# Attention scores of two heads side by side in 64-row halves of TensorE, from two float32r parts

## The chip, the core and the metric

The kernel runs on one core of a Trainium2 chip. The metric is the device time of one launch in microseconds. In the views, PE is TensorE (PEld its weight loads), DVE is VectorE, ACT is ScalarE, POOL is GpSimd and SP is SyncE, whose queue issues the DMAs.

## The reference

One transformer layer with the norms behind: 1024 tokens, width 512, 32 query heads of 16 channels in 8 groups (4 query heads share the keys and values of a group), causal attention, then a linear layer with eight LoRA terms.

```python
q = jnp.dot(x, Wq).reshape(b, t, H, HD).transpose(0, 2, 1, 3)        # H = 32, HD = 16, t = 1024
kv = jnp.dot(x, Wkv).reshape(b, t, G, 2, HD).transpose(2, 3, 0, 1, 4) # G = 8
scores = jnp.einsum('bhqd,bhkd->bhqk', q, k)
scores = jnp.where(causal[None, None], -jnp.inf, scores)
weights = jax.nn.softmax(scores * (1.0 / HD ** 0.5), axis=-1)
ctx = jnp.einsum('bhqk,bhkd->bhqd', weights, v)
# attention: jnp.dot(ctx, Wo) + bo, and then
h = jnp.einsum('bsd,nrd->nbsr', x, lora_A)
coef = (SCALE * lora_weights)[:, None, None]
lora_out = jnp.einsum('nbsr,nor->bso', h, lora_B * coef)
base = jnp.einsum('bsd,od->bso', x, W) + bias
# x = _layernorm(x + attention), then x = _layernorm(x + base + lora_out)
```

## The kernel before

All inputs are float32 and the result is held to float32 accuracy, so narrow types are split into parts whose products are summed. Projections, the output product (WO) and the FFN (FF) take operands in two float32r parts, three products each (`halves`, line 1195). For the scores, query and key are split into three bfloat16 parts, and six products of parts stand below each other as 6 x 16 = 96 rows of the contraction (`ROWS`), so that one matmul of 96 rows makes the scores of a head in full accuracy. `QS` holds these rows for the four heads of a unit, `KS` for the keys of a group. Three more rows (`NROW` = 99) hold the negative row maximum in three bfloat16 parts against rows of ones, so that the scores of the softmax come out with the maximum already subtracted.

The work is cut into 16 units: a unit `u` is four heads of a group and one half (512) of the queries. Units 0 to 7 take the first half, 8 to 15 the second, which sees twice the keys. Each unit passes twice over its scores:

- **Chunks** (`CHUNKS`, `chunk_scores`, line 1135) make scores with the query on the partitions, one matmul a head, up to 512 keys wide. DVE reduces each PSUM bank to a maximum (`chunk_max`: line 910 for a full bank, the fused operation of line 917 with the causal mask for one head of an "own" bank). They run one to three cycles ahead. They take turns in banks 0 to 2 and, where nothing else holds it, bank 7.
- **Cycles** (`CYCLES`, 80 of them) make the scores again with the key on the partitions (`piece_scores`, line 1359, 512 columns each), ACT takes their exponential into `PB` (line 856), on the diagonal POOL zeroes the part above it (line 696), and `accumulate` (line 1337) multiplies `PB` with the values in float32, four heads side by side in 32-column strips of the array. A cycle has four pieces off the diagonal and three on it. A piece has one of the banks 3 to 5 (`ST_BANKS` = 3; from the last unit on six banks).

The order on each engine is written out by the program. TensorE goes through a cycle in four steps, each with a share of the chunks, a piece and a share of the **filler** (`FILL`), the part of another job that goes on beside: projections of the second half, and the T1, T2, WO, T3, FF steps behind the attention of the first half. `accumulate` of the cycle before closes it. How many chunks each cycle takes is planned by `level` from `pe_time` and `dve_time`.

The unit's maxima go DVE (line 931) -> POOL in three parts (`split_maxima`) -> TensorE turns them (line 1143) -> ACT copies (line 744) -> a DMA puts them into `QS` (`move_maxima`, line 507). The first unit does without the DMA: `direct_rows` and `rows_moved` write them straight from PSUM.

A projection of queries or keys ends in `parts`: ACT copies the high part (line 732), DVE subtracts it (line 958), ACT makes the middle part (line 737), POOL the low one (line 582; DVE does it for the first two, line 968). SP then writes `parts` to DRAM (`parts_to_dram`, line 479), waits until it has landed and reads it back in the layout of the rows (`load_queries`, `load_keys`). SP works through this queue strictly in order. The first unit's rows are made by selection matmuls instead (line 1149).

## Time and profile before

| | |
|---|---|
| median of 3 runs | 341.34 us (339.17 to 341.63) |
| the profiled execution: its time, its span | 339.0 us, 337.2 us |
| PE busy | 322.3 us (96%), 2487 matmuls |
| DVE busy | 256.6 us (76%) |
| ACT busy | 216.5 us (64%) |
| POOL busy | 135.3 us (40%) |
| granted clock of TensorE | 0.996 of 2.4 GHz |

Busy time counts a matmul from its issue to its end; matmuls overlap in the pipeline, so a busy PE may still be issuing below its rate. The stages used below are cut at the end of a unit's last `accumulate`: until 36 us the loads, first projections and first chunks, until 100.7 us units 0 to 4, until 128.4 us units 5 to 7, until 265.2 us units 8 to 13 (22.8 us each), until 303.1 us units 14 and 15, then the tail of the second half's WO and FFN. The times of all runs outside the span are 339.0 - 337.2 = 1.8 us.

### The profile page before, as it was taken

How to read it: one execution, taken by the hardware profiler on the slowest of the kernel's cores; microseconds unless marked ns; L12 is line 12 of the kernel's file. 1: busy time of each engine (PE TensorE's matmuls, PEld its weight loads, DVE VectorE, ACT ScalarE, POOL GpSimd, SP SyncE). 2: the span in 40 equal slices, each digit the busy share in tenths (PEclk: the TensorE clock that was granted, in tenths of full speed). 3: DMA queues.
4: the chain of work that ended last, by engine and by line, in shares of the span. 5: the costliest groups of instructions: out<-in, count | busy, mean ns of one | idle time of the engine just before them, and what ended most of it. 6: DMA issues, size and time to landing. Idle time of an engine off the chain costs nothing.

```text
span 337.2 us, 7240 instructions
## 1 busy us (share of the span) xinstructions
PE 322.3 (96%) x2487; PEld 169.7 (50%) x2487; DVE 256.6 (76%) x787; ACT 216.5 (64%) x418; POOL 135.3 (40%) x268
## 2 busy tenths in 40 slices
PE   8999989999999999999999999999999999999992
PEld 3676445455353344454444544544544434558882
DVE  3557968978888899888889889888886961047664
ACT  4754737645657796848757668478585786952431
POOL 8845325433547585347222123212141122331553
PEclk9999999999999999999999999999999999999998
DMA  6886494874244120020010100000000000000002
GB/s 202 289 163 170 132 183 120 225 230 118 53 148 155 36 63 5 3 47 3 3 48 33 48 4 3 0 31 3 3 0 3 32 2 1 2 33 1 0 33 93
DMA packets 16643, 22.96 MB, mean 68 GB/s; under 512 B 3232, under 2 KB 10560, under 8 KB 16608
## 3 DMA queue, kind: packets, MB, share of 16 engines
q1 hardware_dynamic: 16608, 22.51, 24.4%
q8 instruction: 20, 0.33, 0.4%
q14 instruction: 15, 0.12, 0.1%
HBM read 16.29 MB, written 6.03 MB: 66 GB/s over the span
## 4 chain that ended last, share of the span: by engine, by line
PE 71%; DMA 7%; DVE 7%; ACT 4%; issue 4%; SPq 3%; POOL 2%; POOLq 0%; DVEq 0%; ACTq 0%
PE PS L1337 18%; PE PS L1195 16%; PE PS L1135 15%; PE PS L1359 15%; DMA QS<-NMR 3%; ACT PB L856 2%; PE PS L1263 2%; PE PS L1255 2%; DVE scrap L917 2%; DVE MX L910 2%; DMA scr_q<-parts 2%; DMA X<-in_L_attn_x_turned_dram 1%; SPq L490 1%; PE PS L1149 1%; SPq L502 1%
## 5 line engine op out<-in xcount | busy, mean ns | idle before, releaser
L856 ACT ACTIVATE PB<-PS 128x512 f32<-128x512 f32 x288 | 155.6, 604 | 59.1 <-PE PS L1359 57.9
L917 DVE CUSTOM_DVE_ANT_0 scrap<-PS,mask 128x128 bf16<-128x128 f32 (+3 forms) x256 | 111.5, 487 | 17.6 <-PE PS L1135 17.1
L1135 PE MATMUL PS<-KS,QS 96*128 96x512 bf16 (+3 forms) x384 | 107.9, 329 | 2.1 <-DVE MX L910 1.0
L1359 PE MATMUL PS<-QS,KS 99*128 99x512 bf16 x288 | 106.2, 381 | 1.8 <-DMA QS<-NMR 1.4
L910 DVE TENSOR_REDUCE MX<-PS 128x1 f32<-128x512 f32 x128 | 81.9, 684 | 12.4 <-PE PS L1135 11.7
L696 POOL TENSOR_SCALAR_AFFINE_SELECT PB<-PB 128x256 f32<-128x256 f32 (+1 forms) x96 | 46.4, 485 | 104.3 <-ACT PB L856 101.2
L1337 PE MATMUL PS<-PB,VX 128*32 128x256 f32 (+1 forms) x1280 | 78.8, 364 | 0.6 <-ACT PB L856 0.3
L1135 PEld LDWEIGHTS PS<-KS,QS 96*128 96x128 bf16 x384 | 32.9, 98 | 49.4 <-issue 13.6
L1337 PEld LDWEIGHTS PS<-PB,VX 128*32 128x32 f32 x1280 | 33.5, 109 | 41.9 <-issue 19.0
L1195 PE MATMUL PS<-XT,WQ 128*128 128x512 f32 x144 | 45.4, 439 | 0.5 <-ACT NMR L744 0.4
L1359 PEld LDWEIGHTS PS<-QS,KS 99*128 99x128 bf16 x288 | 27.5, 98 | 31.4 <-ACT PB L856 7.9
L1195 PEld LDWEIGHTS PS<-XT,WQ 128*128 128x128 f32 x144 | 26.6, 193 | 9.5 <-DVE XT L1043 1.5
L1195 PE MATMUL PS<-XT 128*128 128x512 f32 x96 | 28.1, 426 | 0.6 <-DVE MX L910 0.6
L1195 PE MATMUL PS<-WQ,XT 128*128 128x512 f32 x96 | 28.3, 427 | 0.0
L677 POOL TENSOR_SCALAR mv<-mv 128x1 f32<-128x1 f32 x15 | 3.4, 228 | 48.7 <-DVE mv L1012 48.6
L917 DVE DVE_READ_ACCUMULATOR2_ANT MX<- 128x1 f32 x256 | 21.2, 83 | 0.0
L1195 PEld LDWEIGHTS PS<-XT 128*128 128x128 f32 x96 | 17.9, 189 | 4.6 <-DVE MX L910 1.1
L1195 PEld LDWEIGHTS PS<-WQ,XT 128*128 128x128 f32 x96 | 17.9, 189 | 4.1
L770 ACT ACTIVATE RAW<-PS 128x256 f32<-128x256 f32 x32 | 12.4, 387 | 11.2 <-PE PS L1337 11.0
L788 ACT ACTIVATE TC<-RAW,shift,rstd 128x512 f32<-128x512 f32 x7 | 5.7, 817 | 13.4 <-POOL shift L679 13.4
L732 ACT ACTIVATE parts<-PS 128x512 bf16<-128x512 f32 x10 | 6.0, 597 | 10.7 <-PE PS L1195 10.7
L658 POOL CAST NMPS<-NM 128x16 bf16<-128x16 f32 x15 | 3.3, 221 | 21.7 <-DVE NM L931 21.7
(93 smaller groups left out, 263.6 us busy)
## 6 DMA issues: line engine op xcount, KB each, us to landing
scr_q<-parts SPq DMA_DIRECT2D x8, 384.0 KB, 4.0
QS<-scr_q SPq DMA_DIRECT2D x15, 192.0 KB, 2.9
X<-in_L_attn_x_turned_dram SPq DMA_DIRECT2D x8, 256.0 KB, 6.3
X<-in_L_attn_x_dram SPq DMA_DIRECT2D x8, 256.0 KB, 3.1
out_dram<-TC SPq DMA_DIRECT2D x8, 256.0 KB, 2.0
QS<-scr_q SPq DMA_DIRECT2D x15, 128.0 KB, 3.0
RAW<-in_L_attn_Wo_dram SPq DMA_DIRECT2D x2, 512.0 KB, 5.9
RAW<-in_L_ffn_W_dram SPq DMA_DIRECT2D x2, 512.0 KB, 9.0
```

The costliest lines, as they stand in the source:

```text
L696: nc.gpsimd.affine_select(out=blk, in_=blk, compare_op=ALU.is_ge, fill=0.0, base=0, pattern=[[0, len(heads)], [1, P]], channel_multiplier=-1)\
L732: nc.scalar.activation(parts[:, m % 2, 0, :], job_bank(n), ACT.Copy).then_inc(act_copied, 1)
L770: nc.scalar.activation(RAW[:, u, cols], PS[:, PV_BANK, cols], ACT.Copy).then_inc(raw_out, 1)
L856: nc.scalar.activation(PB[:, cyc % NP_BUF, k, :], PS[:, score_bank(e), :], ACT.Exp, scale=SCALE)\
L910: nc.vector.tensor_reduce(part[:, j0:j1, 0:1], bank, AX, ALU.max).then_inc(max_read, 1)
L917: last = nc.vector.tensor_tensor_reduce(out=scrap[:, n % 2, (j - j0) * width:(j - j0 + 1) * width], in0=bank[:, j - j0, :], in1=mask[:, HT ...
L1135: last = nc.tensor.matmul(PS[:, CHUNK_BANK[n], k * width:(k + 1) * width], QS[0:ROWS, u % SLOTS, j, qb * P:(qb + 1) * P], KS[0:ROWS, g, k0 ...
L1195: last = nc.tensor.matmul(bank, lhs(a, c), rhs(b, c), start=(k == 0), stop=(k == len(terms) - 1))
L1255: last = nc.tensor.transpose(bank[:, g * P:(g + 1) * P], RAW[:, h * G + g0 + g, qb * P:(qb + 1) * P], ident[:, :])
L1263: last = nc.tensor.transpose(bank[:, c * P:(c + 1) * P], src[:, c * P:(c + 1) * P], ident[:, :])
L1337: last = nc.tensor.matmul(PS[32 * j:32 * j + 32, PV_BANK, s * HQ + skip:(s + 1) * HQ], VX[:, key_blocks(cyc)[i], u % G, :], PB[:, cyc % NP ...
L1359: nc.tensor.matmul(PS[:, score_bank(e), :], KS[0:NROW, u % G, kb * P:(kb + 1) * P], QS[0:NROW, u % SLOTS, heads[0]:heads[-1] + 1, s * HQ + ...
```

## The change

- Query and key are split into two float32r parts instead of three bfloat16 ones. Three products (high x high, high x low, low x high) take 3 x 16 = 48 rows, 51 with the maxima. The middle part on ACT and the low part on POOL (and on DVE for the first two jobs) are gone.
- The 51 rows fit in 64. Of a unit's four heads two stand in rows 0 to 50 and two in rows 64 to 114 of `QS`. `KS` has the keys of one group in the upper and of another in the lower half, and a unit takes two heads of each (`v_group`, and `Wq` and `Wo` are laid out for it ahead of the launch).
- Chunks and pieces are issued in pairs, the first in rows 0 to 63 of the array, the second in rows 64 to 127, into two different banks, with one semaphore increment for both; each pair waits until both banks are free. All score matmuls have float32r operands.
- On the diagonal the one piece of four heads is two pieces of 256 columns, so a cycle has always four pieces; ACT and POOL have four operations there instead of three.
- A long filler comes in two parts of six matmuls, at the first and last step of a cycle, instead of four parts of three; a short one in one part at the last step.
- The first unit's maxima take the DMA as all others do: `move_maxima(0)` stands in SP's queue behind the five `parts_to_dram`, and TensorE waits for it ahead of cycle 0. 16 chunks are due ahead of cycle 0 instead of 14.
- `load_queries` has four DMAs of 2 KB rows for three of 4 KB, `load_keys` four for six, `move_maxima` two for three. `parts` has 512 KB for 384.
- Ones are written into all of `KS` before anything is copied into it, so the copies and loads wait for that constant. In the tail the banks are dealt out anew.

```diff
-    ROWS = 6 * HD
+    ROWS = 3 * HD
     NROW = ROWS + NPART
+    PAIR, TILE = 2, 64
+    Q_TERMS, K_TERMS = (0, 0, 1), (0, 1, 0)
+    def tile_rows(t, count):
+        return slice(t * TILE, t * TILE + count)
+    def v_group(u, j):
+        return (u % G) // 2 + G // 2 * (j // 2)
...
         first = [(0, range(0, 2), 0), (0, range(2, 4), 0)]
-        return first + ([(1, range(0, 4), P)] if on_diagonal(cyc) else [(1, heads, 0) for _, heads, _ in first])
+        return first + [(1, heads, P if on_diagonal(cyc) else 0) for _, heads, _ in first]
...
-        return HT * len(pieces(c)) * (1 + 1.1) / 2.4 + (PE_FILL.get(kind, 2600) if kind else 0)
+        return HT * len(pieces(c)) * (0.6 + 1.1) / 2.4 + (PE_FILL.get(kind, 2600) if kind else 0)
...
-        QS = sb("QS", [P, SLOTS, REP, HT], BF16)
-        KS = sb("KS", [P, G, T], BF16)
+        QS = sb("QS", [P, SLOTS, NPAIR, HT], F32R)
+        KS = sb("KS", [P, G // 2, T], F32R)
...
-        parts = sb("parts", [P, 2, NPART, HT], BF16)
+        parts = sb("parts", [P, 2, 2, HT], F32R)
...
-            load_keys(1, slice(0, G), ks_in[1])
+            move_maxima(0)
+            load_keys(1, slice(0, G // 2), ks_in[1])
...
                 if on_diagonal(cyc):
-                    for k, (_, heads, _) in enumerate(pieces(cyc)):
+                    for k, (_, heads, skip) in enumerate(pieces(cyc)):
...
-            def middle_part(n):
-
-                act.wait_ge(*freed(PROJ[n]))
-                nc.scalar.activation(parts[:, n % 2, 1, :], rest[:, n % 2, :], ACT.Copy).then_inc(rest_split, 1)
...
-                    nc.vector.tensor_tensor(rest[:, s, :], bank, parts[:, s, 0, :], ALU.subtract)\
+                    nc.vector.tensor_tensor(parts[:, s, 1, :], bank, parts[:, s, 0, :].bitcast(F32), ALU.subtract)\
                         .then_inc(job_freed, 1)
...
                 was_read(CHUNK_BEHIND[n])
-                for k, j in enumerate(heads):
-                    last = nc.tensor.matmul(PS[:, CHUNK_BANK[n], k * width:(k + 1) * width],
-                                            QS[0:ROWS, u % SLOTS, j, qb * P:(qb + 1) * P],
-                                            KS[0:ROWS, g, k0:k0 + width], start=True, stop=True)
+                was_read(CHUNK_BEHIND[n + 1])
+                for k in range(len(CHUNKS[n][3])):
+                    for t in range(PAIR):
+                        j = CHUNKS[n + t][3][k]
+                        rows = tile_rows(t, ROWS)
+                        last = nc.tensor.matmul(PS[:, CHUNK_BANK[n + t], k * width:(k + 1) * width],
+                                                QS[rows, u % SLOTS, j % NPAIR, qb * P:(qb + 1) * P],
+                                                KS[rows, v // 2, k0:k0 + width], start=True, stop=True)
                 last.then_inc(max_scores, 1)
...
-                if not long and head % 2 == 0:
+                if head not in ((0, 3) if long else (3,)):
                     return
-                part, parts = (head, REP) if long else (head // 2, 2)
+                part, parts = (head // 3, 2) if long else (0, 1)
...
-                nc.tensor.matmul(PS[:, score_bank(e), :], KS[0:NROW, u % G, kb * P:(kb + 1) * P],
-                                 QS[0:NROW, u % SLOTS, heads[0]:heads[-1] + 1, s * HQ + skip:(s + 1) * HQ],
-                                 start=True, stop=True).then_inc(scores, 1)
+            def pair_scores(cyc, i):
+
+                u, s, _ = CYCLES[cyc]
+                kb = key_blocks(cyc)[i]
+                e = SCORE_BANKS[cyc] + PAIR * i
+                for t in range(PAIR):
+                    bank_free(e + t)
+                for t in range(PAIR):
+                    _, heads, skip = pieces(cyc)[PAIR * i + t]
+                    rows = tile_rows(t, NROW)
+                    last = nc.tensor.matmul(PS[:, score_bank(e + t), 0:len(heads) * (HQ - skip)],
+                                            KS[rows, (u % G) // 2, kb * P:(kb + 1) * P],
+                                            QS[rows, u % SLOTS, :, s * HQ + skip:(s + 1) * HQ], start=True, stop=True)
+                last.then_inc(scores, 1)
...
-                if cyc == 0:
-                    rows_moved()
-                elif cyc == FIRST[u]:
-                    pe.wait_ge(nm_in, 16 * NPART * u)
+                if cyc == FIRST[u]:
+                    pe.wait_ge(nm_in, 16 * PAIR * (u + 1))
```

The order on TensorE in the same cycle (the one in which WO of the first block is the filler, unit 9). Before:

```order
L1337 MATMUL PS<-PB,VX 32x256 x8
L1135 MATMUL PS<-KS,QS 128x256 x2
L1359 MATMUL PS<-QS,KS 128x512
L1195 MATMUL PS<-WQ,XT 128x512 x3
L1135 MATMUL PS<-KS,QS 128x512 x2
L1359 MATMUL PS<-QS,KS 128x512
L1195 MATMUL PS<-WQ,XT 128x512 x3
L1135 MATMUL PS<-KS,QS 128x512
L1359 MATMUL PS<-QS,KS 128x512
L1195 MATMUL PS<-WQ,XT 128x512 x3
L1135 MATMUL PS<-KS,QS 128x512
L1135 MATMUL PS<-KS,QS 128x384
```

And in the changed kernel, where line 1118 is the chunks, 1330 the pieces, 1159 the fillers and 1301 `accumulate`:

```order
L1301 MATMUL PS<-PB,VX 32x256 x8
L1330 MATMUL PS<-QS,KS 128x512 x2
L1159 MATMUL PS<-WQ,XT 128x512 x6
L1118 MATMUL PS<-KS,QS 128x256 x4
L1118 MATMUL PS<-KS,QS 128x512 x2
L1330 MATMUL PS<-QS,KS 128x512 x2
L1118 MATMUL PS<-KS,QS 128x512 x2
L1159 MATMUL PS<-WQ,XT 128x512 x6
L1301 MATMUL PS<-PB,VX 32x256 x4
```

Four single pieces between fillers of three have become two pairs, with a filler of six behind the first and another ahead of `accumulate`.

SP's queue at the start of the attention, from the write of the fourth projection on. Before (line 479 `parts_to_dram`, 502 `load_queries`, 490 `load_keys`, 512 `move_maxima`):

```order
L479 DMA scr_q<-parts 128x3x512
L502 DMA QS<-scr_q 48x2048
L502 DMA QS<-scr_q 32x2048
L502 DMA QS<-scr_q 16x2048
L479 DMA scr_k<-parts 128x3x512
L490 DMA KS<-scr_k 16x8x512 x6
L512 DMA QS<-NMR 1x16x128 x3
```

And in the changed kernel (lines 484, 513, 498, 521 in the same order):

```order
L484 DMA scr_q<-parts 128x2x512
L513 DMA QS<-scr_q 16x1024
L513 DMA QS<-scr_q 32x1024
L513 DMA QS<-scr_q 16x1024
L513 DMA QS<-scr_q 32x1024
L484 DMA scr_k<-parts 128x2x512
L521 DMA QS<-NMR 3x8x128 x2
L498 DMA KS<-scr_k 32x4x512
```

The maxima move of the first unit is new and stands ahead of the keys of the second half, with four query loads where three were. Ahead of these rows stand the write of the third projection and the query loads of two units, now eight DMAs for six.

## Rows read from the trace of the kernel before

**Rows 1.** Busy us (instructions) of PE, PEld, DVE, ACT, POOL by stage; clock; DMA.

```profile
0.00:36.00 36.00, 33.84 (x153) 21.04 (x154) 21.65 (x65) 19.50 (x33) 23.90 (x37) 1.00 0.72 198
36.00:100.70 64.70, 60.86 (x474) 30.63 (x472) 55.20 (x235) 38.86 (x80) 26.19 (x61) 1.00 0.59 155
100.70:128.40 27.70, 27.03 (x245) 11.40 (x234) 25.29 (x76) 22.55 (x49) 20.93 (x35) 1.00 0.28 79
128.40:265.20 136.80, 135.58 (x1158) 65.67 (x1147) 118.41 (x331) 95.75 (x185) 41.13 (x88) 1.00 0.05 14
265.20:303.10 37.90, 36.89 (x347) 18.09 (x337) 14.76 (x40) 29.45 (x58) 10.16 (x23) 1.00 0.04 15
```

**Rows 2.** Groups by line and form: busy us, mean ns, idle before.

```profile
L856 ACT ACTIVATE PB<-PS 128x512 f32<-128x512 f32 x288 | 155.6, 604 | 59.1 <-PE PS L1359 57.9
...
L1337 PE MATMUL PS<-PB,VX 128*32 128x256 f32 x1024 | 71.8, 386 | 0.6 <-ACT PB L856 0.3 <-ACT RAW L770 0.2
...
L1195 PEld LDWEIGHTS PS<-XT,WQ 128*128 128x128 f32 x144 | 26.6, 193 | 9.5 <-DVE XT L1043 1.5 <-ACT NMR L744 1.3 <-ACT XT L815 1.0
...
L770 ACT ACTIVATE RAW<-PS 128x256 f32<-128x256 f32 x32 | 12.4, 387 | 11.2 <-PE PS L1337 11.0
...
L1263 PEld LDWEIGHTS PS<-ident,TC 128*128 128x128 f32 x64 | 8.2, 141 | 4.1 <-DVE MX L910 0.6 <-DVE TC L981 0.4
```

**Rows 3.** The stage 128.4 to 265.2, maxima score matmuls of line 1135 alone.

```profile
128.40:265.20 136.80, 58.89 (x192) 17.02 (x192) 1.00 0.05 14
```

**Rows 4.** The same stage, softmax score matmuls of line 1359 alone.

```profile
128.40:265.20 136.80, 59.42 (x156) 15.25 (x156) 1.00 0.05 14
```

**Rows 5.** The same stage, projection and FFN matmuls of line 1195 alone.

```profile
128.40:265.20 136.80, 25.09 (x72) 13.60 (x72) 1.00 0.05 14
```

**Rows 6.** Chain of waits in order of time: start us, us, what.

```profile
273.63 0.22 PE PS L1263 x2
...
277.24 0.86 PE PS L1359 x4
278.10 1.00 PE PS L1337 x16
279.10 0.32 PE PS L1359
...
281.28 1.38 PE PS L1195 x6
```

**Rows 7.** The same view, early: 128 and 256 columns of line 1135.

```profile
20.40 0.24 PE PS L1135 x4
...
21.63 0.23 PE PS L1135 x2
```

**Rows 8.** Waits, 128.4 to 265.2: who for whom, us, times, longest.

```profile
ACT PB L856 <- PE PS L1359: 33.6, 42, 2.6
...
DVE MX L910 <- PE PS L1135: 10.2, 21, 1.3
```

**Rows 9.** Busy time in the 20 us where VectorE is fullest.

```profile
120.00:140.00 20.00, 19.88 (x181) 8.75 (x178) 18.71 (x55) 16.12 (x33) 12.07 (x19) 1.00 0.08 22
```

**Rows 10.** Timeline of the DMA queue of SyncE: start us, us, what.

```profile
26.09 0.38 SPq L479 DMA_DIRECT2D scr_q<-parts  x1
28.66 2.64 SPq L502 DMA_DIRECT2D QS<-scr_q  x6
31.34 0.42 SPq L479 DMA_DIRECT2D scr_q<-parts  x1
35.30 1.23 SPq L502 DMA_DIRECT2D QS<-scr_q  x3
...
43.94 1.86 SPq L512 DMA_DIRECT2D QS<-NMR  x3
```

**Rows 11.** Timeline of GpSimd, the low part of one projection.

```profile
24.89 1.17 POOL L582 TENSOR_TENSOR parts<-TC,parts 128x512 bf16<-128x512 f32 x1 [1.65 <-ACT parts L737]
```

**Rows 12.** Timeline of TensorE, the first softmax scores.

```profile
36.04 0.38 PE L1359 MATMUL PS<-QS,KS 99*128 99x512 bf16 x1
```

More of the change, by code:

```diff
@@ L15 @@
 EPS = 1e-5
-ONE_ONE = float(np.array([0x3F803F80], np.uint32).view(np.float32)[0])
 ALPHA = 32
@@ L75, in postln_kernel @@
     LAST_OF = {last_of(u, s): (u, s) for u in range(NU) for s in range(2)}
-    def heads_per_bank(width):
-        return min(REP, HT // width) if width <= HT // 2 else 1
     def heads_in_banks(width):
-        n = heads_per_bank(width)
-        return [range(j, j + n) for j in range(0, REP, n)]
+        if width <= HT // 2:
+            return [range(0, 2), range(2, 4)]
+        return [range(j, j + 1) for j in (0, 2, 1, 3)]
     CHUNKS = []
@@ L133, in chunks_of_job @@
         before, due = PLAN_A[n - 1][1] if n else 0, PLAN_A[n][1]
-        a, b = (before + (max(before, due) - before) * p // 3 for p in (part, part + 1))
+        a, b = (before + (due - before) // 2 * p // 3 * 2 for p in (part, part + 1))
         return range(a, b)
@@ L152, in postln_kernel @@
     assert list(FILL) == sorted(FILL)
-    POOL_AT = {c + 1: [("low", PROJ.index(job))] for c, job in FILL.items() if job in PROJ}
+    POOL_AT = {}
     for b in range(TB):
@@ L194, in level @@
             done += r
-            due.append(sum(1 for n in chunks if COST[n + 1] - COST[chunks[0]] <= done + 1))
+            due.append(2 * sum(1 for n in chunks[::2] if COST[n + 2] - COST[chunks[0]] <= done + 1))
         due[-1] = len(chunks)
@@ L275, in postln_kernel @@
     LATE = [(e - WIDE) % ALL_BANKS for e in range(SCORE_BANKS[NCYC - 1], SCORE_BANKS[NCYC])]
-    FREE = [bank for bank in range(ALL_BANKS) if bank not in LATE] + [MISC]
+    FREE = [bank for bank in range(ALL_BANKS) if bank not in LATE] + [MISC, LATE[0]]
+    LATE = LATE[1:]
     assert len(LATE) == 3 and len(FREE) == 4
@@ L852, in _ @@
                     evacuate(*LAST_OF[cyc - 2])
-                for k in range(len(pieces(cyc))):
+                for k, (_, heads, skip) in enumerate(pieces(cyc)):
                     e = SCORE_BANKS[cyc] + k
-                    act.wait_ge(scores, e + 1)
-                    nc.scalar.activation(PB[:, cyc % NP_BUF, k, :], PS[:, score_bank(e), :], ACT.Exp, scale=SCALE)\
-                        .then_inc(probs, 1)
+                    width = len(heads) * (HQ - skip)
+                    act.wait_ge(scores, e // PAIR + 1)
+                    nc.scalar.activation(PB[:, cyc % NP_BUF, k, 0:width], PS[:, score_bank(e), 0:width], ACT.Exp,
+                                         scale=SCALE).then_inc(probs, 1)
                     if k == 0 and cyc == rows_cycle(1) + 1:
@@ L1146, in direct @@
             def direct(lhs, slot, bank):
-                for a in range(NPART):
-                    last = nc.tensor.matmul(PS[0:ROWS, bank, :], lhs[:, a, :], parts[:, slot, a, :],
-                                            start=(a == 0), stop=(a == NPART - 1))
+                for a in range(2):
+                    last = nc.tensor.matmul(PS[:, bank, :], lhs[:, a, :], parts[:, slot, a, :], start=(a == 0),
+                                            stop=(a == 1))
                 last.then_inc(moved, 1)
             def direct_keys():
-                pe.wait_ge(parts_ready, 1)
+                pe.wait_ge(*freed(("K", 0, 0)))
                 pe.wait_ge(sel_ready, 12)
@@ L1295, in _ @@
                     pe_job(n, part)
-                    for k in chunks_of_job(n, part):
+                    for k in chunks_of_job(n, part)[::PAIR]:
                         chunk_scores(k)
@@ L1327, in accumulate @@
                 if on_diagonal(cyc):
-                    pe.wait_ge(masked, 3 * sum(1 for c in LAST_OF if c <= cyc))
+                    pe.wait_ge(masked, 4 * sum(1 for c in LAST_OF if c <= cyc))
                 pe.wait_ge(probs, SCORE_BANKS[cyc + 1])
```

262 lines of the change are left out of this document (113 added, 149 removed).

## The prediction

> **What bounds the kernel now.** I cut the span at the ends of units and read busy times stage by stage [rows 1]. From 36 to 265 us PE is busy 94 to 99% of every stage, DVE 85 to 91%, ACT 60 to 81%. Busy alone proves little on PE, since a matmul counts for its whole flight, so I priced PE by issue, from the chain of waits [rows 6, 7]: four softmax score matmuls in a row take 0.86 us, 0.22 each; two chunks of 256 columns 0.23, 0.115 each; four of 128 columns 0.24, 0.06 each; between 256 and 512 I put 384 columns at 0.165. A float32r matmul of 512 columns takes 1.38 / 6 = 0.23. In the stage of units 8 to 13 (136.8 us) there are 192 chunk matmuls [rows 3] and 156 score matmuls [rows 4]. By the program 120 of the chunks have 512 columns and 24 each have 384, 256 and 128: 120 x 0.22 + 24 x (0.165 + 0.115 + 0.06) = 34.6 us, and 156 x 0.22 = 34.3 us. The 72 filler matmuls [rows 5] take 16.6, the 42 `accumulate` of 1.00 to 1.10 some 44. That is 129 of 136.8 us with transposes still missing: PE is what runs, and the small waits of DVE and ACT for it in this stage (10.2 and 33.6 us) [rows 8] are waits for PE's place in the order. DVE is next: 118.4 us of work in the 136.8 [rows 1].
>
> **Price of a pair.** Nothing before the change shows two row halves. Bounds: `accumulate` has the same arrangement in columns; its 16 float32 matmuls of 386 ns each [rows 2] take 1.00 us together [rows 6], so four strips do run side by side. Then a pair costs one float32r matmul, 0.23. Against it stand the weight loads. One of 128 float32r columns lasts 193 ns [rows 2]. If the second half's load began only when the first's ended, a pair would cost 0.19 + 0.19 + 0.04 (what lies between a load's end and the next matmul, 0.23 - 0.19) = 0.42; with the matmuls in turn as well 0.46. But a load's duration is not its hold on the port: transposes follow each other every 0.11 us [rows 6] while each one's load lasts 141 ns [rows 2], so loads overlap. I take 0.23 for every pair, however narrow, since the load sets it then.
>
> The Trainium skill (TensorEngine Tiling (Array Packing), Key Properties) says that tiles load and multiply in parallel; no run here shows it for rows yet.
>
> **PE, units 8 to 13.** 192 chunks become 96 pairs. Of 42 cycles 12 are on the diagonal, so 156 pieces become 2 x 42 = 84 pairs. 180 x 0.23 = 41.4 for 68.9: 27.5 us less. Half of this comes from the wide ones; a 128-column pair costs 0.23 where it cost 0.12. Added: the array changes its arrangement. Behind an `accumulate` a score matmul takes 0.32 instead of 0.22 [rows 6], so a change costs 0.10. Fillers have 128 rows and had none to pay. A long filler now adds three (in, out, in again ahead of `accumulate`), a short one and the turned maxima one each: 6 x 3 + 12 + 6 = 36, 3.6 us. PE's issue falls from 136.8 to 136.8 - 27.5 + 3.6 = 112.9.
>
> The same page and section says that such a change drains the engine; its sum would be this one.
>
> **What is late next: DVE.** Its operations are the same, 118.4 us here, more than PE's 112.9. The fullest 20 us of the trace have DVE at 18.71, 93.5% [rows 9]; I take that as what it reaches when PE is not in its way. 118.4 / 0.935 = 126.6: the stage gives 10.2 us, not 23.9. At 100% it would give 18.4. ACT has 95.8 + 12 x (2 x 0.387 - 0.604) = 97.8 there, the diagonal's two narrow exponentials priced by the 256-column copy [rows 2]; no bound.
>
> **Units 0 to 4** (64.7 us). A unit has 16 chunk matmuls, 4 of each width, 4 x 0.56 = 2.2 us, now 8 x 0.23 = 1.8; ten pieces, 2.2, now six pairs, 1.4. With 108 chunks and 5 units: -2.6 - 4.1, changes of arrangement +2.0 (5 long fillers, 5 turns): PE 60.0. DVE 55.2 / 0.935 = 59.0 [rows 1, 9]. Both are close, so not the full 4.7: -4. **Units 5 to 7** (27.7 us): DVE 25.3 / 0.935 = 27.0, -0.6. **Units 14 and 15** (37.9 us): no chunks to speak of, 48 pieces into 26 pairs saves 4.6, changes take 1 back. ACT has 29.5 + 0.7, which at the 16.12 of 20 that it reaches at best [rows 9] takes 37.4. Between -0.5 and -3.6 I take -2. **Tail**: 0; nothing in it has scores.
>
> **Start.** Removed on PE: 15 selection matmuls become 6, some 2 us. Removed on the way to SP's writes: the middle part and the low one, 1.17 us on POOL [rows 11], so the third projection's write (26.09) [rows 10] can go some 2 us earlier. But SP's queue is the new path. Cycle 0 now waits for `move_maxima(0)`, and in that queue stand, in this order: that write, 26.09 - 2 = 24.1; its landing, 2.6 us before, up to a third more for 512 KB, 27.2; eight loads of 0.44 (2.64 / 6), 30.7; the next write and its landing, 4.0 to 5.2, 35.3; four loads, 37.0; the write of the keys 37.4; the move, two issues of 0.6 (1.86 / 3) [rows 10], 38.6, and landing. So cycle 0 starts at 38.6 to 41 instead of 36.04 [rows 12], 2.6 to 5 late, and all of PE's work stands behind that wait, the chunks too, so DVE and ACT run dry. Two chunks more are done ahead of it, about 1.5 us of DVE's work, that the later stages need not do. I count +2 (0 to +4).
>
> **Moved or hidden.** POOL has 0.18 us more on each diagonal and 9 less for the low parts; in units 8 to 13 it is busy 30% [rows 1], and the last exponential and its mask are shorter. DMA bytes grow by a third for `parts` only. The extra `KS` constant is on POOL ahead of the first copies.
>
> **Sum.** -10.2 - 4 - 0.6 - 2 + 2 = -14.8 on the profiled execution's 339.0: 324.2. The median is 341.34, 2.3 above this execution; with it 326.5. I say 325.
>
> **Rivals.**
> *The loads of the two halves do not overlap* (0.42 a pair, 0.46 without any concurrency). For: no row shows two 128-column float32r loads in flight. Against: the loads of strips and transposes do. Units 8 to 13: 180 x 0.42 = 75.6 for 68.9 and 3.6 for the changes, +10.3. Units 0 to 4: 84 x 0.42 = 35.3 for 26.1, and 2.0: +11. The rest by the same count +5, start +2: +28, 367 us; at 0.46 about 382. It decides from 0.36 us a pair, where PE's issue is back at 136.8 in units 8 to 13 ((68.9 - 3.6) / 180); up to 0.31 it costs nothing, since DVE is still later. Slower, 15%.
> *The pair costs a buffer.* A pair waits for two free banks of three or four, and all of PE waits behind it. The next pair of pieces may start when the first exponential of the last pair is done; load, gap and flight are 0.19 + 0.04 + 0.38 = 0.61 [rows 2, 12], and the second exponential covers 0.60, so any filler (1.4) or `accumulate` (1.1) in between leaves ACT dry, and its wait comes back to PE. For the maxima, a filler's bank leaves three: a pair then starts after DVE has half finished the one before. If half of the 96 pairs cost DVE 0.3 us, that is 14 us, and the gain is gone: 335 to 343, 17%. Both PE and DVE lose slack here, so it is the likeliest way to be wrong.
> *DVE gets to 100%.* -18.4 - 4.7 - 2.4 - 3.6 and a start at 0: 310 us. 10%.
>
> The Trainium skill (TensorEngine Tiling (Array Packing), PSUM Bottleneck) states that tiling speeds up TensorE and not the emptying of PSUM, which may become the limit. That is the DVE term above; by it alone the gain ends at this rival's 310.
>
> **How the numbers follow.** Forecast case (DVE at 90 to 97%, 316 to 334): 53%. DVE full: 10%. Buffer rival 17%, of which two thirds within 1%. Loads 15%. 5% for a start or a narrow float32r matmul that is dearer than I think, with a time over 345. A measurement of this kernel tells about 1% from no change. Faster 0.68, same 0.12, slower 0.20. The range goes from 310 to the end of the buffer rival, 344; what is outside is the loads case and the 5%.
>
> **What would show it.** Two score matmuls of a pair starting some 10 to 110 ns apart and pairs 0.23 us apart: price right. DVE at 93% or more from 128 us on, with PE's busy share falling to about 90: next bound right. First softmax scores near 39.5 us with PE waiting for the DMA of `NMR`: start right. Units 8 to 13 at 21.1 us each instead of 22.8: the sum right. Wrong if loads follow each other end to end, if ACT's or DVE's waits for score matmuls grow per operation, or if the units' pace stays at 22.8 with no engine over 90%.

## The result and the profile after

The changed kernel takes 431.86 us (median of 4 runs, 429.48 to 436.54) against 340.63 us (339.17 to 341.63) of the kernel before: a ratio of 1.2659, 95% interval 1.2554 to 1.2764. It is 91 us slower. The profiled execution is the slowest of the four, 436.5 us. In the lines of after, 1118 is the chunks, 1330 the pieces, 1159 the fillers, 1301 `accumulate`, 845 the exponentials, 897 and 904 the maxima.

The page of after: busy time of each engine, then its slices.

```profile
PE 356.0 (82%) x2495; PEld 194.7 (45%) x2495; DVE 259.0 (60%) x783; ACT 215.8 (50%) x438; POOL 129.6 (30%) x292
...
PE   7996787877877888778998887788778778989994
...
PEclk9987567898988876995559989989899985799999
```

The same work stands in a longer span. PE fell from 96% to 82%, DVE from 76% to 60%, ACT from 64% to 50%: no engine is full. The granted clock, 1.00 before in all but the last slice, falls again and again.

The stages cut at the ends of the same units as before (columns as in [rows 1]):

```profile
39.90:129.50 89.60, 71.90 (x483) 39.58 (x481) 54.69 (x226) 38.35 (x86) 23.46 (x69) 0.80 0.37 106
129.50:169.20 39.70, 32.75 (x251) 15.07 (x239) 27.66 (x79) 23.15 (x52) 21.04 (x38) 0.76 0.19 59
169.20:351.20 182.00, 146.72 (x1162) 74.13 (x1156) 119.31 (x326) 98.53 (x197) 41.76 (x99) 0.87 0.04 11
351.20:400.80 49.60, 43.00 (x355) 21.42 (x346) 16.23 (x42) 29.94 (x62) 10.55 (x27) 0.79 0.03 11
```

Units 0 to 4 take 89.6 us for 64.7, 5 to 7 take 39.7 for 27.7, 8 to 13 take 182.0 for 136.8, 14 and 15 take 49.6 for 37.9 [rows 1]. DVE's and ACT's work in units 8 to 13 is what it was (119.3 for 118.4, 98.5 for 95.8), so it waits.

The waits of the whole span: who for whom, us, times, longest.

```profile
ACT PB L845 <- PE PS L1330: 111.5, 106, 4.8
PEld PS L1330 <- ACT PB L845: 56.1, 69, 1.3
DVE scrap L904 <- PE PS L1118: 53.3, 49, 3.4
DVE MX L897 <- PE PS L1118: 50.3, 44, 4.4
PE PS L1330 <- ACT PB L845: 30.7, 47, 1.1
PEld PS L1118 <- DVE MX L904: 28.0, 35, 1.7
```

ACT waits 111.5 us for softmax scores, where it waited 57.9 [rows 2]; PE waits for ACT in turn.

TensorE's timeline in unit 12, at full clock there (start us, us, what, [idle before <- releaser]):

```profile
300.45 1.07 PE L1301 MATMUL PS<-PB,VX 128*32 128x256 f32 x16
301.45 0.49 PE L1330 MATMUL PS<-QS,KS 51*128 51x512 f32 x2
301.78 0.40 PE L1118 MATMUL PS<-KS,QS 48*128 48x512 f32 x2
302.79 0.50 PE L1330 MATMUL PS<-QS,KS 51*128 51x512 f32 x2 [0.60 <-ACT PB L845]
303.10 0.47 PE L1118 MATMUL PS<-KS,QS 48*128 48x512 f32 x2
303.50 0.86 PE L1301 MATMUL PS<-PB,VX 128*32 128x256 f32 x16
```

The chain of waits through the same place (start us, us, what):

```profile
301.52 0.45 PE PS L1330 x2
301.96 0.02 issue
301.99 0.02 ACTq L844
302.00 0.04 issue
302.05 0.60 ACT PB L845
302.65 0.14 issue
302.79 0.47 PE PS L1330
```

Two exponentials in a row on ACT's timeline:

```profile
324.80 1.08 ACT L845 ACTIVATE PB<-PS 128x512 f32<-128x512 f32 x2
```

Two matmuls of 512 columns end within 0.49 us: they do run side by side. But from one pair to the next it is 0.31 to 0.33 us (301.45 to 301.78, 302.79 to 303.10), not 0.23. And the chain is a ring, in which each step waits for the one before: pair, first exponential 0.60, 0.14, next pair 0.47, next exponential. The second exponential hides in it, but ACT takes 0.60 + 0.14 + 0.47 + 0.08 = 1.29 us for a pair of pieces whose exponentials take 1.08 back to back, and more wherever anything stands between the pairs.

### The profile page after: what moved, and what is told of

Same layout as the page of the kernel before. It is cut to its first block, busy times and chain, and to the rows that moved or that the text cites. A ratio compares the mean times of both kernels' runs of the same rounds, so it can differ in the third digit from the quotient of the medians.

```text
span 434.8 us, 7602 instructions
## 1 busy us (share of the span) xinstructions
PE 356.0 (82%) x2495; PEld 194.7 (45%) x2495; DVE 259.0 (60%) x783; ACT 215.8 (50%) x438; POOL 129.6 (30%) x292
## 4 chain that ended last, share of the span: by engine, by line
PE 70%; ACT 10%; DVE 9%; issue 8%; DMA 1%; POOL 1%; SPq 0%; POOLq 0%; ACTq 0%; DVEq 0%
PE PS L1159 21%; PE PS L1301 19%; PE PS L1330 13%; PE PS L1118 11%; ACT PB L845 7%; DVE MX L897 4%; DVE scrap L904 3%; PE PS L1227 2%; PE PS L1219 2%; PE PS L1206 1%; DMA X<-in_L_attn_x_turned_dram 1%; ACT RAW L765 1%; DVE MX L904 1%; PE PS L1126 1%; PE PS L1132 0%
## 5 line engine op out<-in xcount | busy, mean ns | idle before, releaser
L845 ACT ACTIVATE PB<-PS 128x512 f32<-128x512 f32 (+1 forms) x320 | 159.6, 558 | 112.9 <-PE PS L1330 111.5
L1330 PE MATMUL PS<-QS,KS 51*128 51x512 f32 (+1 forms) x320 | 82.8, 512 | 32.9 <-ACT PB L845 30.7
L700 POOL TENSOR_SCALAR_AFFINE_SELECT PB<-PB 128x256 f32<-128x256 f32 x128 | 50.2, 407 | 186.8 <-ACT PB L845 183.9
L1118 PE MATMUL PS<-KS,QS 48*128 48x512 f32 (+3 forms) x384 | 77.6, 422 | 33.0 <-DVE MX L904 19.3
L1301 PE MATMUL PS<-PB,VX 128*32 128x256 f32 (+1 forms) x1280 | 95.0, 423 | 1.6 <-ACT RAW L765 0.8
L1330 PEld LDWEIGHTS PS<-QS,KS 51*128 51x128 f32 x320 | 35.4, 207 | 81.3 <-ACT PB L845 56.1
L1118 PEld LDWEIGHTS PS<-KS,QS 48*128 48x128 f32 x384 | 41.2, 208 | 59.0 <-DVE MX L904 28.0
L1159 PEld LDWEIGHTS PS<-XT,WQ 128*128 128x128 f32 x144 | 31.2, 229 | 13.3 <-issue 4.1
L1159 PE MATMUL PS<-WQ,XT 128*128 128x512 f32 x96 | 26.7, 422 | 0.0
L736 ACT ACTIVATE parts<-PS 128x512 fp32r<-128x512 f32 x10 | 6.0, 597 | 27.6 <-PE PS L1159 27.6
L944 DVE TENSOR_TENSOR parts<-PS,parts 128x512 fp32r<-128x512 f32 x10 | 6.9, 691 | 14.7 <-ACT parts L736 14.7
```

What stands on the lines that cost most here:

```text
L700: nc.gpsimd.affine_select(out=blk, in_=blk, compare_op=ALU.is_ge, fill=0.0, base=0, pattern=[[0, len(heads)], [1, P]], channel_multiplier=-1)\
L845: nc.scalar.activation(PB[:, cyc % NP_BUF, k, 0:width], PS[:, score_bank(e), 0:width], ACT.Exp, scale=SCALE).then_inc(probs, 1)
L944: nc.vector.tensor_tensor(parts[:, s, 1, :], bank, parts[:, s, 0, :].bitcast(F32), ALU.subtract)\
L1118: last = nc.tensor.matmul(PS[:, CHUNK_BANK[n + t], k * width:(k + 1) * width], QS[rows, u % SLOTS, j % NPAIR, qb * P:(qb + 1) * P], KS[row ...
L1159: last = nc.tensor.matmul(bank, lhs(a, c), rhs(b, c), start=(k == 0), stop=(k == len(terms) - 1))
L1301: last = nc.tensor.matmul(PS[32 * j:32 * j + 32, PV_BANK, s * HQ + skip:(s + 1) * HQ], VX[:, key_blocks(cyc)[i], v_group(u, j), :], PB[:, ...
```

## The experiments

The pace at full clock is the best measure, since the clock differs from kernel to kernel: in unit 13 TensorE was granted 1.00 throughout wherever a number stands below. Time is the median of all runs of a kernel; "unit 13" and "us at 1.2 GHz", the sum of stretches at that clock, are from its profiled execution.

| kernel | time, us | unit 13, us | us at 1.2 GHz |
|---|---|---|---|
| before | 339.6 | 23.1 | 5 |
| changed | 431.9 | 27.2 | 130 |
| e1 own waits | 398.8 | 26.6 | 51 |
| e2 before, in pairs | 364.4 | 25.3 | 12 |
| e3 pairs twice | 453.8 | 31.4 | 46 |
| e4 filler spread | 431.8 | not at full clock | 158 |
| e5 before, light | 319.5 | 20.7 | 12 |
| e6 halves in turn | 365.0 | 24.3 | 28 |
| e7 own waits, filler spread | 401.0 | not at full clock | 75 |
| e8 two bfloat16 parts | 344.2 | 22.5 | 21 |
| e9 e6 with zeros | 373.7 | 24.3 | 65 |
| e10 one half only | 395.2 | 26.3 | 27 |
| e11 changed, bfloat16 | 394.8 | 25.5 | 61 |
| e12 e8 with zeros | 342.8 | 22.5 | 19 |

In the expectations W is the theory that order and common waits starve ACT and DVE, C that TensorE has too little to do and loses its clock, P that pairs, loads or changes of arrangement are dearer than priced.

**e1: each matmul of a pair waits for its own bank and signals by itself.**

```diff
+                single = len(CHUNKS[n][3]) == 1
                 was_read(CHUNK_BEHIND[n])
-                was_read(CHUNK_BEHIND[n + 1])
+                if not single:
+                    was_read(CHUNK_BEHIND[n + 1])
...
                 for t in range(PAIR):
                     bank_free(e + t)
-                for t in range(PAIR):
...
-                last.then_inc(scores, 1)
+                    last.then_inc(scores, 1)
```

> The changed kernel, but each score matmul of a pair waits for its own bank alone and signals for itself; row halves, float32r parts, fillers and plan stay. Theory W (the pair's common wait and signal empties ACT and DVE): 30 to 50 us of the 91 us loss come back (380 to 400 us), units 8 to 13 go from about 30 us to about 25. Theory C (the clock is the loss, through the array having less to do): PE's order stays as thin, so the clock is still at half for some 100 us and the time stays over 420 us. Theory P (a pair costs 0.33 us instead of 0.23 through its loads): no change beyond 5 us.

Measured 398.8 us (ratio to before 1.174, 1.166 to 1.182), 33 less than the changed kernel. The time is in W's range. But unit 13 went from 27.2 only to 26.6: at full clock the waits of single banks are worth 0.6 us a unit. Most of the 33 is clock: the profiled executions differ by 79 us at 1.2 GHz.

**e2: the kernel before (bfloat16, 99 rows, no halves), its chunks and pieces two at a time, with one wait for both banks and one signal.**

```diff
-        return [lot[len(lot) * q // 4:len(lot) * (q + 1) // 4] for q in range(4)]
+        half = len(lot) // 2
+        return [lot[:half], lot[:0], lot[half:], lot[:0]]
...
-                        piece_scores(cyc, j)
+                    if j % 2 == 0:
+                        both = j + 1 < len(pieces(cyc))
+                        piece_scores(cyc, j, [0, 1] if both else [0], 0 if both else 1)
+                        if both:
+                            piece_scores(cyc, j + 1, [], 2)
```

> The kernel before (bfloat16, 96 and 99 rows, no halves), but pieces and chunks are issued two at a time: the first waits for both banks, both signal at the second. Theory W: this alone costs much of the loss with the array's work as before: 360 to 390 us. Theory C: the matmuls are all still there, so little falls, 340 to 350 us, clock 1.0. Theory P: 340 to 345 us.

Measured 364.4 us (ratio 1.073, 1.062 to 1.084). It is W's range. No instruction in it works on anything else than before, so 25 us are the price of the grouping alone, the 7 us more at 1.2 GHz with it. Its units 8 to 13 take 149.6 us for 136.7, cut in the same way in both: 13 of the 25 us. Its waits:

```profile
ACT PB L857 <- PE PS L1365: 94.2, 115, 4.7
DVE scrap L918 <- PE PS L1139: 30.5, 44, 3.2
DVE MX L911 <- PE PS L1139: 24.5, 46, 2.1
```

ACT's wait goes from 57.9 [rows 2] to 94.2 with the grouping alone.

**e5: the kernel before with half the columns of the wide score matmuls from cycle 8 on.** It leaves half of the scores out.

```diff
+                    part = width // 2 if width == HT and n >= DUE[8] else width
...
+                cut = len(heads) // 2 if cyc >= 8 else len(heads)
```

> The kernel before with single waits, but from cycle 8 on the softmax score matmuls and the 512-column maxima matmuls stream only half of their columns (the other half of each bank keeps older scores), so that PE has about as much less to do as the pairs should save, 45 to 50 us of issue. ACT and DVE work as before. Theory W: with the order of waits intact the gain comes, DVE becomes the limit, 318 to 328 us. Theory C: the thinner array lets the clock fall, the granted clock is under 0.95 and the time is 335 us or more. Theory P says as W, since no pair and no long load is in it.

Measured 319.5 us (ratio 0.941, 0.933 to 0.948). This is what the prediction hoped for: TensorE relieved, order and waits as before. From 124 to 247 us, nearly its units 8 to 13:

```profile
124.00:247.00 123.00, 113.87 (x1170) 62.50 (x1168) 117.70 (x339) 95.50 (x189) 44.37 (x91) 1.00 0.07 19
```

DVE is busy 117.7 of 123.0 us, 96%, and the bound. Its own units 8 to 13 take 120.7 us, 20.1 each, for 22.8. So the next bound was named rightly; it was the relief that did not come. C's forecast, a clock under 0.95 and 335 us or more, failed (0.984 and 0.995).

**e3: every wide pair of chunks and every pair of pieces is issued twice.**

```diff
-                    for t in range(PAIR):
+                    for t in (0, 1, 0, 1) if width == HT else (0, 1):
...
-                for t in range(PAIR):
+                for t in (0, 1, 0, 1):
```

> The changed kernel with every 512-column pair and every pair of pieces issued twice in a row (the second overwrites the first with the same scores; one signal as before). PE gets about 65 us more issue at full clock. Theory C: the array stays busy enough to keep the clock at 0.98 or more, and the time falls, to 400 us or less, in spite of the added work. Theory W: the added 0.22 us stands in the path from each wait to its signal, and the time rises to 445 us or more.

Measured 453.8 us (449.1 and 458.6), as W said. The stretches at 1.2 GHz shrank from 130 to 46 us, and still it is 22 us slower: more work kept the clock up but cost more than it brought. In units 8 to 13, 84 + 60 pairs are added for (31.4 - 27.2) x 6 = 25 us, 0.17 us each, half of what a pair costs. That fits a TensorE that was partly waiting, partly full.

**e6: halves and float32r as in the changed kernel, order as before.** Four steps a cycle, single chunks and pieces, own waits and signals, halves taken in turn, fillers in four or two parts.

```diff
-            return [range(0, 2), range(2, 4)]
-        return [range(j, j + 1) for j in (0, 2, 1, 3)]
+            return [range(2, 4), range(0, 2)]
+        return [range(j, j + 1) for j in (2, 0, 3, 1)]
...
+            def piece_scores(cyc, k):
...
+                bank_free(e)
+                rows = tile_rows(k % 2, NROW)
...
-                if head not in ((0, 3) if long else (3,)):
+                if not long and head % 2 == 0:
```

> Data layout, float32r parts and row halves of the changed kernel, but the order of the kernel before: four steps a cycle, in each single chunks and one piece, each waits for its own bank and signals for itself, fillers in four parts, chunks planned singly. Neighbours on PE stand in different row halves (chunks begin with the second half, pieces with the first), so they can still run side by side where both are free to start. Theory W (what is lost is the order in which ACT and DVE are fed, not the halves): 320 to 345 us, units 8 to 13 at 20.5 to 23 us. Theory C (the thinner array loses its clock whatever the order): over 360 us with a granted clock under 0.93. Theory P (float32r loads and changes of arrangement are dearer than I priced): 350 to 370 us with the clock near 1.

Measured 365.0 us (ratio 1.074, 1.069 to 1.079), 67 less than the changed kernel; unit 13 takes 24.3 for 27.2. W's 320 to 345 us were missed: the order gives back most of the loss, but not all, and what is left is in the range of P. TensorE's timeline (columns as above):

```profile
156.47 0.50 PE L1325 MATMUL PS<-QS,KS 51*128 51x512 f32 x1
156.48 0.73 PE L1115 MATMUL PS<-KS,QS 48*128 48x512 f32 x2
156.82 0.52 PE L1325 MATMUL PS<-QS,KS 51*128 51x512 f32 x2
157.06 0.40 PE L1115 MATMUL PS<-KS,QS 48*128 48x256 f32 x2
```

A piece and a chunk in different halves start 0.01 us apart without being issued as a pair; the next two come 0.34 us later.

**e7 and e4: the fillers in four or two parts again, in e1 and in the changed kernel.**

```diff
-                if head not in ((0, 3) if long else (3,)):
-                    return
-                part, parts = (head // 3, 2) if long else (0, 1)
+                if not long and head % 2 == 0:
+                    return
+                part, parts = (head, REP) if long else (head // 2, 2)
```

> The kernel with own waits and signals (399 us) and, further, the fillers in four parts (long) and two parts (short) as before the change. Theory W: a filler of six matmuls in one piece holds ACT and DVE up for 1.4 us twice in 20 of 80 cycles; spread it gives back 5 to 15 us, 384 to 394. Theory P: each more part costs two more changes of arrangement, 0.1 to 0.2 us each, so 2 to 6 us slower than 399.

> The changed kernel with only its fillers in four and two parts again, waits and signals still in pairs. Theory W: 5 to 15 us less than 432. Theory C: more breaks of the array's arrangement and no less waiting, so 430 to 440.

Measured 401.0 us against 398.8, and 431.8 against 431.9: the 5 to 15 us that W forecast did not come back. The clock hides something here, though. The profiled executions have 25 us (e7) and 28 us (e4) more at 1.2 GHz than the kernels that they are compared with. At full clock e7's units 10 and 12 take 25.4 us for 26.8 in e1's unit 8, and its units 9 and 11 take 27.2 for 26.7 in e1. So spread fillers give back some 0.4 us a unit on the mean, and the long ones are a small part of the cause. What remains from e7 to e6 is 1.7 us in even units (25.4 to 23.7) and 2.8 in odd ones (27.2 to 24.4). This leaves one thing for it: score matmuls two at a time at two places of a cycle, instead of singly at four.

**e8: e6 with both parts bfloat16 instead of float32r** (`QS`, `KS`, `parts`, `NMR`, `scr_q`, `scr_k`).

```diff
-        QS = sb("QS", [P, SLOTS, NPAIR, HT], F32R)
-        KS = sb("KS", [P, G // 2, T], F32R)
+        QS = sb("QS", [P, SLOTS, NPAIR, HT], BF16)
+        KS = sb("KS", [P, G // 2, T], BF16)
```

> The halves in turn with the order and waits of before (365.0 us), but the two parts are bfloat16 instead of float32r (rows, loads, selection and the DRAM copy; 48 and 51 rows in 64-row halves as before). It leaves out accuracy: the scores then hold only the two highest parts of each number. It asks whether what is left over the kernel before (25 us) is the price of float32r operands (P: loads of 183 ns instead of about 90, 0.49 us to the end of a fresh matmul instead of 0.38, 0.33 us between two neighbours) or of the row halves themselves. P says units 8 to 13 go from 23.7-24.5 us to 21 to 22.5, the time to 340 to 350. If it is the halves (change of arrangement, waits of two neighbours for each other's column), units stay at 23.5 to 24.5 and the time at 360 to 365; only the smaller DMAs at the start can then take a microsecond off.

Measured 344.2 us (ratio 1.015, 1.008 to 1.022), 21 less than e6; unit 13 takes 22.5 for 24.3. TensorE's timeline in e8:

```profile
147.49 0.39 PE L1325 MATMUL PS<-QS,KS 51*128 51x512 bf16 x1
147.49 0.60 PE L1115 MATMUL PS<-KS,QS 48*128 48x512 bf16 x2
147.72 0.49 PE L1325 MATMUL PS<-QS,KS 51*128 51x512 bf16 x2
147.94 0.38 PE L1115 MATMUL PS<-KS,QS 48*128 48x256 bf16 x2
```

Its weight loads of the pieces, from the groups by form (busy us, mean ns | idle):

```profile
L1325 PEld LDWEIGHTS PS<-QS,KS 51*128 51x128 bf16 x320 | 25.0, 95 | 31.2 <-ACT PB L845 20.9 <-issue 6.9
```

and e6's:

```profile
L1325 PEld LDWEIGHTS PS<-QS,KS 51*128 51x128 f32 x320 | 52.1, 191 | 26.0 <-ACT PB L845 17.4 <-issue 7.2
```

With bfloat16 two neighbours go every 0.22 us (147.49, 147.72, 147.94), with float32r every 0.34. A load takes 95 ns for 191. Over the whole trace the median from two neighbours of 512 columns to the next two is 0.226 us in e8, 0.338 in e6, 0.337 in the changed kernel. Time and units came out as P forecast.

**e10: e6 with every score matmul in rows 0 to 50.**

```diff
-                    rows = tile_rows(j // NPAIR, ROWS)
+                    rows = tile_rows(0, ROWS)
```

> The halves in turn again (365.0 us), but every score matmul, of chunks and of pieces, reads rows 0 to 50 and none rows 64 to 114, so no two can run side by side; counts, columns, waits and the changes of arrangement are the same. The heads of the lower half get the scores of the upper half, so the output is another function's. It asks what running side by side is worth in this order. If it is worth what a free pair shows (0.33 us for two instead of 2 x 0.23), and TensorE is what runs, 174 pairs in units 8 to 13 cost up to 0.13 us more each, 23 us, 3.8 us a unit: units at 26 to 28 us and a time of 385 to 400. If the two neighbours are mostly kept apart by waits for banks and by other work between them, it is worth little: units at 23.5 to 25 us and 362 to 372.

Measured 395.2 us (ratio 1.151, 1.142 to 1.160), in the first of the two ranges. The two of its four runs with e6's clock (0.968 and 0.964) took 390.2 and 391.5, 26 more than e6; unit 13 takes 26.3 for 24.3. Singles then follow each other every 0.24 us:

```profile
265.19 0.40 PE L1115 MATMUL PS<-KS,QS 48*128 48x512 f32 x1
265.43 0.39 PE L1325 MATMUL PS<-QS,KS 51*128 51x512 f32 x1
265.66 0.39 PE L1115 MATMUL PS<-KS,QS 48*128 48x512 f32 x1
```

So running side by side is real and worth some 2 us a unit; a float32r pair at 0.34 saves 0.14 on two singles at 0.24, where the prediction counted 0.21 (0.23 for twice 0.22).

**e11: the changed kernel with bfloat16 parts** (the edit of e8).

> The changed kernel (431.9 us) with one edit: the two parts are bfloat16 instead of float32r, everything else (pairs with one wait and one signal, blocks of two, fillers of six) as in it. It leaves out accuracy: the scores hold only the two highest parts. In the kernel with the order and waits of before the same edit was worth 20.7 us (365.0 to 344.2). If the two causes only add (the data type by its own price, the order by W), this one falls by 15 to 25 us, to 407 to 417, and ACT's and DVE's waits for score matmuls stay above 90 and 70 us. If it is float32r that made the waits of a pair long (0.49 us of flight and 0.19 of load behind each), it falls by 35 to 60 us, to 372 to 397, units 8 to 13 to 25 us, and the stretches of 1.2 GHz nearly vanish.

Measured 394.8 us (ratio 1.164, 1.157 to 1.171), 37 less. Unit 13 takes 25.5 for 27.2, a step of 1.7, as from e6 to e8 (1.8). From e11 to e8 the order is worth 3.0, from the changed kernel to e6 2.9. At full clock the two causes simply add; the 16 us by which 37 exceeds 21 go with the 69 us at 1.2 GHz that e11 has less. The expectation was half met: the time fell further than its 15 to 25 us for causes that only add, and ACT's wait for softmax scores fell to 81.0 us, under its 90.

**e9 and e12: twelve, and ten, matmuls of zeros ahead of TensorE's wait for unit 0's maxima, in e6 and in e8.**

```diff
+            pe.wait_ge(*freed(FIRST_BEHIND[PV_BANK]))
+            for _ in range(IDLE):
+                nc.tensor.matmul(PS[:, PV_BANK, :], Z[:, 0:P], Z[:, :], start=True, stop=True)
```

> The halves in turn again (365.0 us), with twelve matmuls of zeros (512 bfloat16 columns each, into the bank that accumulate uses first) ahead of TensorE's wait for the maxima of unit 0, where it stood idle for 2.9 us before 37.8 us and then ran at 1.2 GHz for 21 us. C says the idle stretch is what lets the clock fall: with it filled the granted clock stays at 1.00 through unit 0, unit 0 takes 15.5 to 17 us instead of 22.5, and the time falls by 5 to 8 us, to 357 to 360. If the clock falls for what unit 0 itself does, the half-clock stretch and the 365 stay.

> The halves in turn with two bfloat16 parts (344.2 us; accuracy left out as there), with ten matmuls of zeros ahead of TensorE's wait for the maxima of unit 0, where TensorE stood idle for 2.0 us before 36.5 us and then ran at 1.2 GHz for 17 us. In the float32r kernel the same edit did not stop that, and the wait there outlasted the twelve matmuls by 1.9 us. Here ten of them (2.2 us) end about when the wait does. If standing idle right ahead of cycle 0 is what lets the clock fall, it stays at 1.00, unit 0 takes 15.5 to 16.5 us instead of 19.9, and the time is 339 to 341, level with the kernel before. If not, 343 to 347.

e9 took 360.9 to 382.9 us in four runs, at mean granted clocks of 0.984 to 0.918. The zeros ended 1.9 us before the wait did:

```profile
35.88 2.75 PE L1332 MATMUL PS<-Z 128*128 128x512 bf16 x12 [0.34 <-ACT TC L725]
40.52 0.44 PE L1115 MATMUL PS<-KS,QS 48*128 48x384 f32 x1 [1.89 <-DMA QS<-NMR]
```

In the profiled run the clock was at 1.2 GHz from 42.3 us for 34 us all the same, and twice more later. In e12 the zeros closed the gap and unit 0 took 14.4 us for 19.9 at a clock of 1.00, but in the profiled run unit 4 ran 13.7 us at half clock instead (19.7 us for e8's 13.7). e12's median is 342.8 us (340.4 to 349.4 in 10 runs; the two at clocks of 0.992 and 0.993 took 340.4 and 340.8). The 339 to 341 us that were expected of it did not come. In ten profiled executions, those of the changed kernel and of all versions with rows in halves but e12, TensorE stood idle for 1.9 to 3.8 us right ahead of cycle 0, and the clock fell to 1.2 GHz during that or within 2 us behind it; in e12's, with no such gap, it did not. So the gap goes with the fall there, and filling it does not keep the clock up elsewhere. These runs also give its price: from 0.984 to 0.918 the time at 1.2 GHz goes from 2 x 0.016 x 359 = 11.5 us to 2 x 0.082 x 381 = 62.5, and the time grows by 22 us, 0.43 us for each us at half clock. In the changed kernel unit 9, with 29.2 us at half clock, took 37.2 us for unit 13's 27.2: 0.35.

## Why the prediction was wrong, point by point

**The steps that failed.** First, the time of a stage was taken as its fullest engine's work (DVE at 93.5%), with 13.7 us of slack on PE for whatever else might come; scores two at a time with common waits took 13 to 17 us of the largest stage, and only a rival had them. Second, a wide float32r pair was put at 0.23 us; it takes 0.34. Third, the clock was left at 1.00 throughout, without a reason given; 125 us more at 1.2 GHz cost about half of the loss.

**Where the loss is.** The profiled executions (436.5 and 339.0 us) are 97.5 us apart. The changed one has 125 us more at 1.2 GHz; at 0.35 to 0.43 each that is 44 to 54 us, an estimate from the two rows above. The rest, 43 to 54, stands at full clock: 4.1 us in unit 13 (27.2 for 23.1; 25 us if units 8 to 13 are alike), 3.4 at the start, what remains in the other units. Of unit 13's 4.1, the order is 2.9 (e6), float32r 1.8 (e8), and the halves themselves with two bfloat16 parts -0.6.

**The pair at 0.23 us failed for wide float32r pairs.** The step took "0.23 for every pair, however narrow, since the load sets it then". Measured from pair to pair at 512 columns: 0.34 for float32r, 0.23 for bfloat16. The narrow float32r pairs were no dearer than priced: in the changed kernel, e1, e3, e4 and e7 those of 256 columns took 0.22 in the median and those of 128 took 0.06 to 0.17, so the load alone does not set the price. Units 8 to 13 have 132 pairs with 512 columns, 24 with 256, 12 with 128 and 12 with 384, which took 0.25 to 0.35 in the few rows that have them. With the 3.6 for changes the same sum reads 58 to 60 us against 68.9, an estimate, and PE's issue would have been 125 to 128 us for 136.8: level with the 126.6 that was forecast from DVE. So the price of a pair by itself would hardly have moved the forecast of this stage. What failed with it is the slack behind DVE that should have paid for it: with the waits of before, float32r costs 1.8 us a unit (e6 against e8), where that slack would have made it free. The bounds (0.23 to 0.42) held the wide pair; the choice of the lower end failed. It rested on the strips of `accumulate` and on transposes, whose loads last 141 ns [rows 2]; the float32r load of 128 columns, 193 ns [rows 2], was in hand, and no row had two of them in flight. The threshold "up to 0.31 it costs nothing" is, by these widths, where the mean pair came to lie (0.30 to 0.31), and it did cost.

**That two halves run side by side held.** In the changed kernel 275 of 352 pairs start 0.01 us or less apart and none over 0.07, and e10 loses 26 us without it.

**A change of arrangement at 0.10 held, except into a filler.** Medians from start to start over the trace: from a score matmul to transposes 0.32 us in e8 for 0.22 before, from a transpose to scores 0.20 for 0.11, from a filler to scores 0.33 for 0.24. Behind float32r neighbours the next filler starts after 0.43 (e6), which is their 0.34 and 0.09 for the change. Into a filler it is more: from a score matmul to the filler's second matmul 0.65 for 0.46, so 0.19. It matters for e8, which changes at four places of each cycle: in its units 8 to 13 there are 24 changes from scores to fillers, 24 to transposes and 18 back from each, some 10 us by these medians, an estimate. This is a likely reason why its 22.5 us in unit 13 are hardly better than the 23.1 of before, though 114 of its pairs in units 8 to 13 run together. That was not tried apart.

**"DVE is next" held, but was never reached** (e5). Its 93.5% was even low: 96%.

**The rival "The pair costs a buffer" had the right mechanism, and nearly the right price in its stage.** It gave 14 us in units 8 to 13, from DVE alone, and nothing elsewhere. There e2 measures 13 on a kernel without any slower instruction, and from the changed kernel to e6 it is 2.9 x 6 = 17 at full clock, if all six units are like unit 13. What it had wrong is the rest: it set the 14 against a gain that did not come, it left out the other stages (e2 loses 25 us in all), and it left out the clock, with which the order is worth 67 us (e6). "ACT: no bound" was true of its work and wrong of its waits: 111.5 us for 57.9. The prediction had the ring in hand (0.61 covered by 0.60) and judged it by what covers the wait in the best case; with float32r the flight, from a matmul's start to its end, is 0.49, not 0.38, and the cover is gone even then.

The Trainium skill (TensorEngine Tiling (Array Packing), PSUM Bottleneck) says that tiling speeds the array up but not the emptying of PSUM. The traces agree in direction: ACT's and DVE's work stayed at 98.5 and 119.3 us in units 8 to 13. What made the time at full clock was not the emptying itself but banks given and taken in twos, and the dearer float32r pairs.

**The clock was not in the sum.** The kernel before had 1.00 up to its last slice, and the prediction treated that as given. The granted clock of the changed kernel, whose TensorE is busy 81% of units 8 to 13 (146.7 of 182.0) where it was busy 99% [rows 1], fell to 1.2 GHz fifteen times, for the first long time at 37.5 us, in TensorE's wait of 2.1 us ahead of cycle 0. It was worth about half of the loss, by the estimate above. The Trainium skill (TensorE: Matmul & The Clock Gate, Part 1) says that the clock follows how busy the array has been; e12's unit 0 agrees (14.4 us with the gap filled, 19.9 without), e12's unit 4 shows that this gap is not the whole rule, and what lowers the clock in a given unit stays open.

**The start held.** First exponential at 39.9 us for 36.5, 3.4 later, inside the 2.6 to 5; SP's queue after:

```profile
25.75 3.56 SPq L513 DMA_DIRECT2D QS<-scr_q  x8
29.54 0.38 SPq L484 DMA_DIRECT2D scr_q<-parts  x1
32.74 1.90 SPq L513 DMA_DIRECT2D QS<-scr_q  x4
34.68 0.42 SPq L484 DMA_DIRECT2D scr_k<-parts  x1
35.87 1.67 SPq L521 DMA_DIRECT2D QS<-NMR  x2
```

The eight loads end at 29.3 (predicted 30.7), the four at 34.6 (37.0), the move at 37.5 (38.6). Its second price, unit 0 at half clock, was missing.

**The range.** 344 was the end of the buffer rival at 14 us. Its 17% and the 15% for dear loads were both partly true at once, and no case let them add up or let the clock follow.

No version here is faster than the kernel before but e5, which leaves half of the scores out. e12 comes nearest, at 342.8 us, with less accuracy.

## What to carry to other kernels

Before two instructions are tied to one wait and one signal, write down the ring through the buffers at its worst, with the flight time of the new operand type, and price every us in which the consumer misses its cover on both engines; here the grouping alone cost 25 us on an unchanged kernel (e2). Price an unseen combination of type and tile at the upper bound unless a row shows that type and that tile width: bfloat16 pairs kept 0.23 us, float32r pairs of 512 columns took 0.34. Do not let the slack of an engine pay for a new cost when that engine gives every other one its place in the order: the sum gave PE 13.7 us of slack, and float32r cost 1.8 us a unit all the same. And when the plan makes the busiest engine wait, count its clock too: here a stretch at 1.2 GHz cost 0.35 to 0.43 of its length, and the changed kernel had 125 us more of them than before.

## What the runs showed of the hardware that was not expected

- Two float32r matmuls of 64-row halves start 0.01 us or less apart even when they come from different code and are not issued as a pair, but the next two follow after 0.34 us, where two bfloat16 ones follow after 0.23 and single float32r ones in one half after 0.24. Narrow float32r pairs follow faster: 0.22 us at 256 columns, 0.06 to 0.17 at 128.
- A fresh float32r score matmul of 51 rows and 512 columns lasts 0.49 us to its end, a bfloat16 one 0.38 to 0.39, and float32r weight loads of 128 columns last 191 ns against 95, with 51 rows or with 128.
- From a score matmul in a half to the second matmul of a full-height filler it is 0.65 us (e8), for 0.46 where both have the full height (before).
- The granted clock fell to 1.2 GHz ahead of the last slice in every profiled version other than the kernel before, also in e10, whose TensorE is busy 97% of the span against 96% before; with the same kernel (e9) the mean clock differed from run to run between 0.918 and 0.984, and the time by 22 us.
